# A causal attention block: the diagonal's first 64 queries of two heads share columns, and the token shift is mixed ahead of single products

## The chip, the cores and the metric

The kernel runs on one core of a Trainium2 chip. The metric is device time in microseconds (us) from start to end of the program on that core, as the median of several runs. Lower is better.

## What is computed

A batch of 8 sequences of 512 tokens and 128 channels goes through one attention layer with 16 heads of 8 channels, a residual and a layer norm, then through a channel mix with a token shift, a residual and a second layer norm. Cut to what matters:

```python
raw    = einsum('bhid,bhjd->bhij', q, k)
scores = alpha * tanh(raw / beta) + lam * hamming + lat      # two biases from 6-bit features
attn   = softmax(where(causal, scores, -inf))                # (8, 16, 512, 512), i >= j only
out    = einsum('bhij,bhjd->bhid', attn, v) @ out_w.T
x      = layernorm(x + out)
x_prev = concat([0, x[:, :-1]], axis=1)                      # the token before
xr     = mu_r * x + (1 - mu_r) * x_prev
xk     = mu_k * x + (1 - mu_k) * x_prev
r      = sigmoid(xr @ W_r.T)
kv     = square(relu(xk @ W_k.T)) @ W_v.T
x      = layernorm(x + r * kv)
```

## The kernel before

**Tiling.** A batch is one period of 20 steps. `P` is 128. For each head the kernel holds the scores transposed, keys on the partitions and queries on the columns. The 512 keys form 4 blocks (`jb`) of 128, and block `jb` is computed for queries `128*jb` to 512 alone: 512, 384, 256 and 128 columns, 1280 per head. Four heads form a quad, and the 5120 columns of a quad are packed into 5 pairs of PSUM banks of 1024 columns (`pair_units`), so a batch has 20 pairs. In each block the first 128 queries are the diagonal one, of which half is masked away.

**A pair's way.** TensorE makes the raw scores of pair `t+1` (`scores`, bf16 in three levels, contraction 72), ScalarE takes their tanh into `probs` (`tanh`), TensorE overwrites the bank with the two biases (`biases`, contraction 111), VectorE adds `alpha * tanh` to them (`main`, L1073), ScalarE takes exp (`exp`, L834, three steps later), GpSimd zeroes the masked triangle (`mask`, L962), and TensorE multiplies with the values (`weighted`, f32, four heads side by side in four strips of 32 output rows of the bank `sums`). There are three PSUM pairs for the raw scores and 10 buffers for `probs`.

**Side work.** Between the pairs run the side products of other batches through one bank (`side_bank`): for batch b+2 the transpose of x, q, k and the two feature products (`xT2`, `q2`, `k2`, `F2`, `G2`), for batch b+1 the values (`v1`), for batch b-1 the end of the layer (`oT0`, `oT1`, `aT`, `y`, `x1T`, `kk`, `rr`, `kv`). The tables `PREP_UNITS`, `VALUES_UNITS`, `POST_UNITS`, `VALUES_STEPS` and the `PREP`, `POST` and `SPLIT` tables of VectorE and GpSimd say in which step each engine does what; each engine runs its own list in order and waits on semaphores. `kk` and `rr` apply the token shift inside the product: the weights come twice, scaled by mu and by 1-mu (`w_k_mix`, `w_r_mix`), and the product of the token and that of the token before are added in PSUM.

**Three levels.** Each of Q, K, J and G is split in three bf16 levels: `hi` (VectorE cast), `rest` (GpSimd, the f32 remainder), `mid` (VectorE cast of it, L1112), `lo` (GpSimd). They go to DRAM and come back as the stacks `q_stack`, `k_stack`, `i_stack`, `j_stack` for the batch (SyncE, `write_rows` and `load_stacks`). The bias of a batch's first pair waits for the last of these loads.

**The ends.** Ahead of batch 0 stands a set-up with the first two batches' preparation. Batch 6 has no preparation left to do, batch 7 none and no values either, and after it comes the tail: the last pairs' exp, mask and product, and the end of the layer for batch 7, cut in halves.

## Time and profile before

| | us |
|---|---|
| median of 3 runs | 400.71 |
| lowest, highest | 400.51, 401.08 |
| the profiled execution | 402.91 |
| its span, first to last instruction | 401.2 |
| TensorE's granted clock, mean share of full speed | 0.979 |
| busy in the span: PE, DVE, ACT, POOL | 361.6, 333.0, 327.9, 229.8 |

PE is TensorE, PEld its weight loads, DVE is VectorE, ACT is ScalarE, POOL is GpSimd and SP is SyncE. Each row of a timeline is one instruction or a run of equal ones: its start, its length, the engine, the line, what it writes and reads, how many. In square brackets stands the idle time of the engine ahead of it, and what ended it. Starts of neighbouring rows tell more than their lengths on PE, because matmuls overlap.

### The profile page before, as it was taken

The page shows a single profiled execution, that of the slowest core. Times are in us where ns is not written, and L with a number is a line of the kernel's source. Part 1 is how long each engine was busy: PE and PEld are TensorE (multiplying, and loading weights), DVE is VectorE, ACT ScalarE, POOL GpSimd, SP SyncE. Part 2 cuts the span into 40 slices and gives each one's busy share as a digit, 9 for nine tenths or more (in the row PEclk, how much of TensorE's full clock was granted, in tenths as well). Part 3 has the DMA queues.
Part 4 walks back from the last instruction along what each step waited for, and adds up shares of the span by engine and source line. Part 5 has one row for each costly group of instructions (what it writes and reads, how often), then busy time and mean ns, then how long its engine had stood idle before and what let it go on. Part 6 is the DMA issues. An engine that isn't in the chain of part 4 may idle for free.

```text
span 401.2 us, 9042 instructions
## 1 busy us (share of the span) xinstructions
PE 361.6 (90%) x3045; PEld 209.1 (52%) x3045; DVE 333.0 (83%) x536; ACT 327.9 (82%) x367; POOL 229.8 (57%) x367
## 2 busy tenths in 40 slices
PE   7788878489999999999999999999989998989983
PEld 7473433134665565655564556455634564445572
DVE  4878979348999999989999999999978977797654
ACT  1216899538998999899999999899989998999811
POOL 4516557314578648765777567956684537344542
PEclk9999999859999999999999999999999999999998
DMA  4264786787613576357544763475337630100000
GB/s 127 72 192 144 233 235 177 205 236 174 155 59 116 159 196 176 100 157 189 154 139 128 203 158 116 146 204 159 117 116 209 174 95 2 54 26 3 2 28 26
DMA packets 37809, 53.76 MB, mean 134 GB/s; under 512 B 3523, under 2 KB 35267, under 8 KB 36191
## 3 DMA queue, kind: packets, MB, share of 16 engines
q1 hardware_dynamic: 32909, 50.83, 45.9%
q10 hardware_dynamic: 4865, 2.49, 2.5%
q8 instruction: 19, 0.31, 0.3%
q14 instruction: 16, 0.12, 0.1%
HBM read 38.69 MB, written 14.61 MB: 133 GB/s over the span
## 4 chain that ended last, share of the span: by engine, by line
PE 54%; DVE 12%; ACT 10%; issue 7%; DMA 6%; SPq 6%; POOL 4%; POOLq 0%; DVEq 0%; ACTq 0%
PE raw L521 25%; PE side_bank L521 13%; PE sums L521 12%; DMA i_stack<-hamming_i 5%; ACT probs L829 4%; DVE probs L1073 4%; ACT probs L834 4%; PE side_bank L613 3%; SPq L387 2%; POOL parts L975 2%; POOL res L1003 1%; DVE bn L1158 1%; DMA probs<-in_L_attn_hex_w 1%; SPq L403 1%; ACT k_act L846 1%
## 5 line engine op out<-in xcount | busy, mean ns | idle before, releaser
L1073 DVE SCALAR_TENSOR_TENSOR probs<-probs,scal,raw 128x1024 f32<-128x1024 f32 x160 | 202.3, 1273 | 35.6 <-PE raw L521 35.0
L829 ACT ACTIVATE probs<-raw 128x1024 f32<-128x1024 f32 x160 | 164.4, 1028 | 33.0 <-PE raw L521 30.6
L834 ACT ACTIVATE probs<-probs 128x1024 f32<-128x1024 f32 x160 | 169.8, 1063 | 0.3 <-DVE probs L1073 0.3
L962 POOL TENSOR_SCALAR_AFFINE_SELECT probs<-probs 128x256 f32<-128x256 f32 (+1 forms) x224 | 97.2, 450 | 114.0 <-ACT probs L834 113.6
L521 PE MATMUL raw<-i_stack,j_stack 111*128 111x384 bf16 (+3 forms) x512 | 97.8, 303 | 11.7 <-DMA i_stack<-hamming_i 7.8
L521 PE MATMUL raw<-q_stack,k_stack 72*128 72x384 bf16 (+3 forms) x512 | 97.8, 303 | 9.6 <-DVE probs L1073 7.5
L521 PE MATMUL sums<-probs,values 128*32 128x256 f32 (+2 forms) x1280 | 82.4, 384 | 0.4 <-POOL probs L962 0.4
L521 PEld LDWEIGHTS raw<-q_stack,k_stack 72*128 72x128 bf16 x512 | 42.4, 98 | 58.8 <-DVE probs L1073 27.4
L521 PEld LDWEIGHTS raw<-i_stack,j_stack 111*128 111x128 bf16 x512 | 41.4, 98 | 55.8 <-issue 22.6
L521 PEld LDWEIGHTS sums<-probs,values 128*32 128x32 f32 x1280 | 33.8, 109 | 30.2 <-issue 20.0
L975 POOL TENSOR_TENSOR parts<-whole,parts 128x512 bf16<-128x512 f32 x30 | 35.6, 1195 | 3.8 <-DVE parts L1112 3.1
L969 POOL TENSOR_TENSOR whole<-whole,parts 128x512 f32<-128x512 f32 x22 | 26.9, 1223 | 11.1 <-DVE parts L1107 11.1
L521 PE MATMUL sums<-ident 128*128 128x128 f32 x118 | 16.8, 296 | 1.6 <-POOL ident L941 1.6
L1112 DVE CAST parts<-whole 128x512 bf16<-128x512 f32 x31 | 18.2, 602 | 0.0
L521 PEld LDWEIGHTS sums<-ident 128*128 128x128 f32 x118 | 15.9, 211 | 3.0 <-POOL ident L941 1.6
L985 POOL TENSOR_TENSOR rstd<-var_eps,minus_half 128x4 f32<-128x4 f32 x14 | 14.7, 1047 | 1.2
L521 PEld LDWEIGHTS side_bank<-w_r_mix,x1T 128*128 128x128 f32 x112 | 13.1, 191 | 1.9 <-ACT k_act L846 1.9
L521 PE MATMUL side_bank<-w_r_mix,x1T 128*128 128x128 f32 x112 | 13.9, 277 | 0.0
L969 POOL TENSOR_TENSOR whole<-feats,parts 128x512 f32<-128x512 f32 x8 | 9.5, 1186 | 6.9 <-DVE parts L1107 6.9
L1003 POOL TENSOR_TENSOR res<-gated,x 128x512 f32<-128x512 f32 x7 | 9.0, 1289 | 7.6 <-DVE gated L1179 7.6
L1158 DVE BATCH_NORM_STATS2 bn<-res 128x6 f32<-128x128 f32 x56 | 12.2, 281 | 1.3 <-POOL res L1003 1.1
L521 PE MATMUL side_bank<-x1T,w_k_mix 128*128 128x512 f32 x28 | 13.2, 592 | 0.0
(154 smaller groups left out, 347.8 us busy)
## 6 DMA issues: line engine op xcount, KB each, us to landing
q_stack<-q_rows SPq DMA_DIRECT2D x21, 384.0 KB
k_stack<-k_rows SPq DMA_DIRECT2D x21, 384.0 KB
i_stack<-lattice_i SPq DMA_DIRECT2D x21, 288.0 KB
i_stack<-hamming_i SPq DMA_DIRECT2D x21, 288.0 KB
q_rows<-parts SPq DMA_DIRECT2D x8, 384.0 KB, 4.3
k_rows<-parts SPq DMA_DIRECT2D x8, 384.0 KB, 2.6
k_rows<-parts SPq DMA_DIRECT2D x8, 256.0 KB, 2.9
x_res<-in_L_attn_x SPq DMA_DIRECT2D x8, 256.0 KB, 3.0
```

Of the source, the lines that this page charges most:

```text
L521: return nc.tensor.matmul(o, lhsT, rhs, start=start, stop=stop, **kw)
L613: last = nc.tensor.transpose(o[:, n * P:(n + 1) * P], src(n), ident[:])
L829: nc.scalar.activation(pair_probs(t), raw[:, t % PSUM_PAIRS, :].rearrange("p (u i) -> p u i", u=2), ACT.Tanh).then_inc(tanh_done, 1)
L834: nc.scalar.activation(pair_probs(t), pair_probs(t), ACT.Exp).then_inc(exp_done, 1)
L962: last = nc.gpsimd.affine_select(out=v, in_=v, compare_op=ALU.is_ge, fill=0.0, base=0, pattern=[[0, v.shape[1]], [1, P]], channel_multipli ...
L969: nc.gpsimd.tensor_tensor(whole[:, kind, :], feats[:] if kind == J else whole[:, kind, :], parts[:, kind, 0, :], ALU.subtract).then_inc(re ...
L975: nc.gpsimd.tensor_tensor(parts[:, kind, 2, :], whole[:, kind, :], parts[:, kind, 1, :], ALU.subtract).then_inc(lo_done[kind], 1)
L985: nc.gpsimd.tensor_tensor(rstd[:], var_eps[:], minus_half[:], ALU.pow).then_inc(rstd_done, 1)
L1003: nc.gpsimd.tensor_tensor(res[:], gated[:], x1[:], ALU.add).then_inc(gate_done, 1)
L1073: v.scalar_tensor_tensor(out=o, in0=o, scalar=scal[:, 2:3], in1=raw[:, t % PSUM_PAIRS, :].rearrange("p (u i) -> p u i", u=2), op0=ALU.mult ...
L1112: v.tensor_copy(parts[:, kind, 1, :], whole[:, kind, :]).then_inc(mid_done[kind], 1)
L1158: v.bn_stats(bn[:, blk, :], res[:, blk, :]).then_inc(bn_done, 1)
```

## The change

**Packing.** A key block's last 64 keys are masked for the block's first 64 queries. The 128-key products therefore leave these queries out: a head has 448, 320, 192 and 64 columns, 1024 in all, two heads fill a pair, and a batch has 16 such pairs. What is left, 64 keys by 64 queries for each block and head, is a square. Eight heads' squares fill one pair (`is_square`, the 9th and the 18th of a batch): the first quad's on partitions 0 to 63, the second's on partitions 64 to 127, with the same columns. A batch has 18 pairs in place of 20. A square pair takes 32 products of 64 keys by 64 columns for the scores, 8 of 64 by 256 for the biases, and 16 for the values, with a value tile that holds the two heads below each other (`square_values`, filled by two more VectorE copies of 64 partitions). Its mask is a GpSimd product with a 0/1 tile (`triangle`, 128x1024); the others' masks are two selects of 2x64 columns each, in place of one or two of 2x128 or 4x128.

**Token shift.** GpSimd subtracts the token before from the token (`shift_diff`, 128x512), VectorE multiplies by mu and adds (`mixed`, twice), and `kk` and `rr` become one product each in place of two. The tail keeps the old form, with weights scaled by four VectorE instructions there.

**Splitting.** In the steady periods `mid` moves from VectorE's cast to GpSimd, which computes the same remainder a second time with a bf16 output.

**Order.** All tables are new for 18 steps. `sums_out` comes behind `main`, and GpSimd makes its constants in the set-up (`square_constants`).

```diff
-PAIRS_PER_QUAD = 5
-PAIRS = QUADS * PAIRS_PER_QUAD
+HALF_PAIRS = 9
+PAIRS = 2 * HALF_PAIRS
+SQUARE = 64
...
+                if is_square(t):
+                    for jb in range(JB):
+                        for r in range(4):
+                            for s in range(2):
+                                first_key = square_heads(t, s)[r] * T + jb * P
+                                at = 4 * SQUARE * jb + SQUARE * r
+                                last = mm(raw[SQUARE * s:SQUARE * (s + 1), t % PSUM_PAIRS, at:at + SQUARE],
+                                          k_stack[par][:, first_key:first_key + SQUARE],
+                                          q_stack[par][:, first_key:first_key + SQUARE])
+                else:
+                    for u, bank in enumerate(pair_units(t)):
+                        for h, jb, at in bank:
+                            n = T - jb * P - SQUARE
...
+                if is_square(t):
+                    squares = pair_probs(t).rearrange("p u i -> p (u i)")
+                    for jb in range(JB):
+                        for r in range(4):
+                            at = 4 * SQUARE * jb + SQUARE * r
+                            last = mm(sums[32 * r:32 * r + 32, jb * P:jb * P + SQUARE],
+                                      square_values[par][:, jb, 4 * k + r, :], squares[:, at:at + SQUARE],
+                                      start=False, stop=(jb == JB - 1), skip_group_check=True)
...
-                    mm(o, w_k_mix[0][:], x1T[:, 1:1 + T], stop=False)
-                    last = mm(o, w_k_mix[1][:], x1T[:, 0:T], start=False)
+                    pe.wait_ge(mix_done[1], pv + 1)
+                    last = mm(o, w_kT[:], mixed_in[1])
...
+                    nc.gpsimd.tensor_tensor(v, v, triangle[:].unsqueeze(1).broadcast_to([P, 2 * T // SQUARE, SQUARE]),
+                                            ALU.mult).then_inc(mask_done, 1)
...
+                for at in (0, SQUARE if p < 2 else P + SQUARE):
+                    block = v[:, :, at:at + SQUARE]
+                    last = nc.gpsimd.affine_select(out=block, in_=block, compare_op=ALU.is_ge, fill=0.0, base=SQUARE,
+                                                   pattern=[[0, 2], [1, SQUARE]], channel_multiplier=-1)
...
+            def mid(n, kind):
+
+                pool.wait_ge(hi_done[kind], n + 1)
+                nc.gpsimd.tensor_tensor(parts[:, kind, 1, :], feats[:] if kind == J else whole[:, kind, :],
+                                        parts[:, kind, 0, :], ALU.subtract).then_inc(mid_done[kind], 1)
...
+            def mixed(n, which):
+
+                dve.wait_ge(dif_done, n + 1)
+                v.scalar_tensor_tensor(out=mixed_in[which], in0=shift_dif, scalar=mu[:, which:which + 1],
+                                       in1=x1T[:, 0:T], op0=ALU.mult, op1=ALU.add).then_inc(mix_done[which], 1)
```

Before, PE in a steady period around the token shift's products (steps 16 and 17; the row with `w_k_mix` is `kk`, the one with `w_r_mix` is `rr`; the REGISTER_ALU rows set up waits):

```order
L521 MATMUL side_bank<-x1T,w_k_mix 128x512 x2
L521 MATMUL raw<-q_stack,k_stack 128x384
L521 MATMUL raw<-q_stack,k_stack 128x128
L521 MATMUL raw<-q_stack,k_stack 128x384
L521 MATMUL raw<-q_stack,k_stack 128x128
L562 REGISTER_ALU
L521 MATMUL raw<-i_stack,j_stack 128x512 x2
L622 REGISTER_ALU
L521 MATMUL side_bank<-w_r_mix,x1T 128x128 x8
```

Now, PE at the same products (steps 13 and 14; `k_act` and `r_tanh` hold the mixed input there):

```order
L540 MATMUL side_bank<-k_act,w_kT 128x512
L590 REGISTER_ALU
L540 MATMUL raw<-i_stack,j_stack 128x64
L540 MATMUL raw<-i_stack,j_stack 128x448
L540 MATMUL raw<-i_stack,j_stack 128x64
L540 MATMUL raw<-i_stack,j_stack 128x448
L540 MATMUL raw<-q_stack,k_stack 128x192
L540 MATMUL raw<-q_stack,k_stack 128x320
L540 MATMUL raw<-q_stack,k_stack 128x192
L540 MATMUL raw<-q_stack,k_stack 128x320
L664 REGISTER_ALU
L540 MATMUL side_bank<-w_rT,r_tanh 128x128 x4
```

The two products are halved, and each pair's blocks are 64 columns shorter, with 64-column blocks among them. The square pair's scores are one run of 32 small products, which stands on PE in steps 7 and 16 of a period, ahead of another pair's biases:

```order
L540 MATMUL side_bank<-woT,attnT 128x128 x4
L540 MATMUL raw<-q_stack,k_stack 64x64 x32
L590 REGISTER_ALU
L540 MATMUL raw<-i_stack,j_stack 128x192
L540 MATMUL raw<-i_stack,j_stack 128x320
```

Before, POOL from the first layer norm on (`x` is the normalised x1) to the third level of Q and the remainder of G, steps 11 to 14:

```order
L993 TENSOR_TENSOR x<-res,mean_var 128x512
L997 TENSOR_TENSOR x<-x,rstd 128x512
L959 REGISTER_ALU
L962 AFFINE_SELECT probs<-probs 128x4x128
L959 REGISTER_ALU
L962 AFFINE_SELECT probs<-probs 128x2x128
L959 REGISTER_ALU
L962 AFFINE_SELECT probs<-probs 128x2x128
L975 TENSOR_TENSOR parts<-whole,parts 128x512
L969 TENSOR_TENSOR whole<-whole,parts 128x512
```

Now, POOL from the same place, steps 9 to 11 (L1036 is `mid` of K, L1071 `shift_diff`, L1018 the square's mask):

```order
L1061 TENSOR_TENSOR x<-res,mean_var 128x512
L1065 TENSOR_TENSOR x<-x,rstd 128x512
L1014 REGISTER_ALU
L1023 AFFINE_SELECT probs<-probs 128x2x64 x2
L1036 TENSOR_TENSOR parts<-whole,parts 128x512
L1070 ISA
L1071 TENSOR_TENSOR gated<-x1T 128x512
L1014 REGISTER_ALU
L1018 TENSOR_TENSOR probs<-probs,triangle 128x1024
L1030 TENSOR_TENSOR whole<-whole,parts 128x512
L1043 TENSOR_TENSOR parts<-whole,parts 128x512
```

Between the layer norm and the next remainder GpSimd now also has the second level, the shift's difference and a mask over 1024 columns.

## Rows read from the trace of the kernel before

**Rows 1.** Windows: stretch and length, busy us per engine, clock, DMA share, GB/s
```profile
core 0: us, PE busy (x) PEld busy (x) DVE busy (x) ACT busy (x) POOL busy (x), PEclk, DMA share, GB/s
...
159.70:201.80 42.10, 41.01 (x360) 23.39 (x358) 39.47 (x60) 39.81 (x44) 29.14 (x45) 1.00 0.58 155
...
328.00:372.00 44.00, 40.55 (x365) 22.77 (x362) 33.93 (x47) 41.97 (x47) 20.37 (x39) 1.00 0.07 20
```

**Rows 2.** Timeline of PE where batch 1's first biases wait (start, length)
```profile
74.03 0.60 PE L521 MATMUL raw<-q_stack,k_stack 72*128 72x512 bf16 x2
81.85 1.03 PE L521 MATMUL raw<-i_stack,j_stack 111*128 111x512 bf16 x2 [7.21 <-DMA i_stack<-hamming_i]
```

**Rows 3.** Windows: the stretch of the low clock
```profile
77.00:90.50 13.50, 8.65 (x24) 3.85 (x24) 4.64 (x5) 3.83 (x4) 1.61 (x4) 0.51 0.88 243
```

**Rows 4.** Timeline of PE: `kk` in periods 1, 5 and 7
```profile
115.78 1.88 PE L521 MATMUL side_bank<-x1T,w_k_mix 128*128 128x512 f32 x4
...
284.36 1.88 PE L521 MATMUL side_bank<-x1T,w_k_mix 128*128 128x512 f32 x4
...
367.02 1.88 PE L521 MATMUL side_bank<-x1T,w_k_mix 128*128 128x512 f32 x4
```

**Rows 5.** Timeline of PE in steady periods: `rr`, scores, biases, products with the values
```profile
202.92 1.95 PE L521 MATMUL side_bank<-w_r_mix,x1T 128*128 128x128 f32 x16
...
207.24 0.60 PE L521 MATMUL raw<-i_stack,j_stack 111*128 111x384 bf16 x4
207.77 1.72 PE L521 MATMUL sums<-probs,values 128*32 128x256 f32 x24
209.42 0.61 PE L521 MATMUL raw<-q_stack,k_stack 72*128 72x512 bf16 x2
...
213.92 0.60 PE L521 MATMUL raw<-q_stack,k_stack 72*128 72x384 bf16 x4
214.35 0.60 PE L521 MATMUL raw<-i_stack,j_stack 111*128 111x512 bf16 x2
```

**Rows 6.** Timeline of PE in the set-up: the smallest products
```profile
12.53 0.46 PE L521 MATMUL raw<-twT,tr_sb 7*6 7x16 f32 x12
```

**Rows 7.** Groups of PEld by form, whole span: busy and mean ns behind the bar
```profile
L521 PEld LDWEIGHTS raw<-q_stack,k_stack 72*128 72x128 bf16 x512 | 42.4, 98 | 58.8 <-DVE probs L1073 27.4 <-issue 17.9 <-DVE w_k_mix L1238 0.2
...
L521 PEld LDWEIGHTS sums<-probs,values 128*32 128x32 f32 x1280 | 33.8, 109 | 30.2 <-issue 20.0 <-POOL probs L962 2.3
```

**Rows 8.** Timeline of ACT in period 7: one tanh to the next
```profile
363.50 1.04 ACT L829 ACTIVATE probs<-raw 128x1024 f32<-128x1024 f32 x1
364.41 1.07 ACT L834 ACTIVATE probs<-probs 128x1024 f32<-128x1024 f32 x1
365.35 1.04 ACT L829 ACTIVATE probs<-raw 128x1024 f32<-128x1024 f32 x1
```

**Rows 9.** Groups of DVE by form in the stretch 159.7 to 201.8
```profile
L1073 DVE SCALAR_TENSOR_TENSOR probs<-probs,scal,raw 128x1024 f32<-128x1024 f32 x20 | 25.4, 1272 | 1.7 <-PE raw L521 1.4 <-ACT probs L829 0.3
L1112 DVE CAST parts<-whole 128x512 bf16<-128x512 f32 x4 | 2.6, 663 | 0.0
...
L1107 DVE CAST parts<-whole 128x512 bf16<-128x512 f32 x3 | 1.4, 488 | 0.0
...
L1107 DVE CAST parts<-feats 128x512 bf16<-128x512 f32 x1 | 1.1, 1144 | 0.0
...
L1124 DVE COPY values<-side_bank 128x256 f32<-128x256 f32 x2 | 0.8, 420 | 0.0
...
L1170 DVE TENSOR_TENSOR res<-side_bank,x_res 128x512 f32<-128x512 f32 x1 | 0.7, 690 | 0.2 <-PE side_bank L521 0.2
```

**Rows 10.** Groups of POOL by form in the same stretch
```profile
L962 POOL TENSOR_SCALAR_AFFINE_SELECT probs<-probs 128x256 f32<-128x256 f32 x24 | 9.8, 425 | 8.6 <-ACT probs L834 8.6
L975 POOL TENSOR_TENSOR parts<-whole,parts 128x512 bf16<-128x512 f32 x4 | 4.8, 1204 | 0.0
...
L962 POOL TENSOR_SCALAR_AFFINE_SELECT probs<-probs 128x512 f32<-128x512 f32 x4 | 2.6, 640 | 1.8 <-ACT probs L834 1.8
```

**Rows 11.** Timeline of the tail: the last mask, and the last product with the values
```profile
379.86 0.64 POOL L962 TENSOR_SCALAR_AFFINE_SELECT probs<-probs 128x512 f32<-128x512 f32 x1 [0.63 <-ACT probs L834]
...
380.55 0.64 PE L521 MATMUL sums<-probs,values 128*32 128x256 f32 x8 [0.19 <-POOL probs L962]
```

226 lines of the change are left out of this document (132 added, 94 removed).

## The prediction

> **What bounds the kernel now.** I read the windows first. In a steady period (one batch, 42.1 us) PE is busy 41.0 us, ACT 39.8, DVE 39.5 and POOL 29.1 [rows 1]. PE has 1.1 us to spare, so PE sets the period, and ACT and DVE, 2.3 and 2.6 us behind, come next. In the last periods, without preparation, ACT is the busiest: 41.97 of 44.0 us [rows 1]. Second, the landmarks. The product `kk` stands in the same step of each period, at 115.78, 284.36 and 367.02 [rows 4]. Periods 1 to 5 are thus (284.36 - 115.78)/4 = 42.1 us each (2.1 a step), and the two behind them (367.02 - 284.36)/2 = 41.3. Third, the start: PE is through with batch 0 at about 74.6 and then stands 7.2 us, until the last load of batch 1's stacks has landed at 81.85 [rows 2], and the clock is at about half until 90.5 [rows 3]. What is saved ahead of 81.85 therefore only makes that wait longer. The sum is made against this execution's span of 401.2; its own time was 402.9 and the median is 400.7, so I take the difference of the spans off the median.
>
> **PE, a steady period: what goes.** Scores lose 256 columns for each of 16 heads, four blocks of 1024. Such a block takes 0.43 us from start to start (213.92 to 214.35 [rows 5]), so 1.7 us go. The biases lose the same, 1.7. In the product with the values four heads run side by side; the 24 matmuls at 207.77 are 896 columns of four heads (two blocks of 256, one of 384) and the next work starts 1.65 later [rows 5]. That is 1.55 without the change of tile shape (below), or 1.7 ns a column; 256 columns for four quads are 1.8. `kk` and `rr` are halved: (1.88 + 1.95)/2 = 1.9 [rows 4, 5]. Together 7.1 us go.
>
> **PE: what comes.** *Change of tile shape.* The biases at 207.24 need 0.43, yet the values' product behind them starts 0.53 later [rows 5]: 0.1 us for going from 128 output rows to 32, and I take as much for going back. Each of a square's two runs in 64-row tiles pays 0.2. *The square's scores*, 32 products of 64 by 64. The trace has no 64-row tile. From below: the two halves run side by side as the values' four strips do, and 16 times 64 columns at 0.43 ns are 0.43, so 0.6 with the changes. From above: a load (98 ns, the 128-wide row of [rows 7]) bare in front of each of the 32, 3.1, so 3.3. Twelve products of 16 columns took 0.46 [rows 6], 26 ns from start to start once the last one's own length is off; 32 of these are 0.8. I take 1.0, since that row is the nearest. *The square's biases*, 8 products of 256 columns: 4 x 107 ns side by side or 8 x 107 in a row, with the changes 0.6 to 1.05; I take 0.6. *Its product with the values*: two passes of 4 blocks of 64 columns, 0.45 if the columns count, 0.9 if the load (109 ns [rows 7]) does; I take 0.55. A square pair is 2.15, two are 4.3. *The 64-column blocks* of the other pairs (16 in the scores, 16 in the biases, 4 in the values' product) may be shorter than the load that runs beside them: 0 to 1.3 us a period, I take 0.5. Net: -7.1 + 4.3 + 0.5 = -2.3.
>
> A rule of the Trainium skill speaks against this part. TensorEngine Tiling (Restrictions) says that column tiling switches Fast Weight Load off, so 64-wide bf16 loads would not be as quick as the 128-wide ones here; TensorE: Matmul & The Clock Gate (LDWEIGHTS) puts such a load at columns/1.2 ns, by which an estimate is 53 ns for 64. By that the 32 scores would be 16 x 53 = 0.85 us if the halves overlap and 1.7 if not, in place of my 0.8. No row of this trace has such a load.
>
> **The other engines in the same period.** ACT: one tanh to the next is 1.85 us when it is not held up [rows 8], so two steps fewer are -3.7. DVE: two `main` fewer are -2.5, four casts fewer -2.65, two more value copies +0.8 (0.42 each, the price of the two that stand there), `mixed` twice between 0.69 (a two-input operation of that size) and 1.14 (the dearest of that size) each [rows 9], I take +1.8: net -2.5, to about 37. The same cast took 1.144 from `feats` and 0.488 from `whole` [rows 9], the first beside GpSimd work; with GpSimd busier the other three casts may cost up to 2 us more. GPSIMD Engine Reference (Specifications), of the Trainium skill, states such contention for DVE instructions in a two-port mode or with two SBUF inputs, and `mixed` has two; by it both `mixed` are at their upper price, 0.5 us over my sum. POOL: the selects leave 12.4 and bring 32 x 0.32 = 10.2 (two sizes, 425 and 640 ns, put 128 columns at about 0.32), two square masks of twice 1.2 are +4.8, four `mid` +4.8, `shift_diff` +1.2 [rows 10]: 29.1 becomes 37.7.
>
> **The period.** PE's 41.0 - 2.3 = 38.7, with its 1.1 of slack 39.8. Now DVE and POOL both stand at 37 to 38 with waits in between, where POOL had 13 us of air; I add 0.3: 40.1 us, 2.23 a step.
>
> **The whole.** Batch 0's two steps are hidden by the load that ends at 81.85; it would cost about 4 us if that cover were gone, and no instruction ahead of that load is moved (GpSimd's new constants, some 3 us, fall into its idle time in the set-up). From 81.85 to `kk` of period 1 it was 33.9 us for 15 steps, 2.3 over 15 x 2.1, the price of the low clock. Now 12 steps: 26.8 + 2.3, so `kk` at 111.0. Four periods of 40.1: 271.4. The next two were 41.3, where ACT's own work is 20 x 1.85 + 1.85 for `kk` and `rr` = 38.9, 2.4 less; now 18 x 1.85 + 1.85 + 2.4 = 37.6 each: 346.6. Behind the last `kk` there were 34.2 us (401.2 - 367.0). Now one step more stands there (+2.1), `kk` and `rr` are shorter (-1.9), and the last pair is a square: its mask is 2.4 instead of 0.64 on the path to the end [rows 11], and its products cost 0.2 more: 36.4. The tail's four weight instructions lie beside the last exp. The end is at 383.0, 18.2 earlier, and the median 382.5.
>
> **Rivals.**
> *GpSimd sets the period.* It works in order, and its list makes it wait: `mid` of G stands ahead of a mask and needs a VectorE cast that is two steps further on in VectorE's list; `shift_diff` waits for the copy of `x1T`, and behind it `mixed` holds VectorE, `main` and so the next scores. For it: 37.7 of 40.1. Against: most masks have two steps until they are needed. With 3.6 us of waits the period is 41.3: 1.2 x 4.7 periods more, 388.1.
> *The squares cost more than they free*, the slower side. Each of the 32 loads stays bare: 3.3 + 1.05 + 0.9 = 5.25 a square, 6.2 us more a period than in the sum, in about 5.7 periods (the last two have slack on PE): 382.5 + 35 = 418. It decides from 1.6 us over my 2.15, that is about 75 ns for each small score product in place of 26. Against: 32-row loads of four strips do overlap, or 24 matmuls with a mean load of 109 ns would not fit into 1.65 us.
> *Better.* The halves overlap fully (0.6 + 0.6 + 0.45), short blocks cost nothing, nobody else interferes: PE 37.2, and POOL's 37.7 with a us of waits sets 38.8: 1.3 x 4.7 off, 376.4.
> *It doesn't arrive.* The wait at 81.85 moves, because batch 1's stacks are written or fetched later, or the clock stays low longer after the now longer stand (about 11 us): 3 to 8 us more, up to 391.
>
> **How the numbers follow.** The forecast (378.5 to 387) 0.52, GpSimd 0.20, better 0.13, the start 0.06, squares too dear 0.08, and 0.01 for an end within 0.2% of before, about what a measurement of this kernel can tell from no change. Faster 0.90, same 0.02, slower 0.08. The range takes in the better case and GpSimd's with the unit costs' width (the squares' scores from 0.6 to 1.7 move the end by -4 to +8): 375 to 392.
>
> **What would show it.** Right: `kk` of periods 1 and 5 some 160 us apart; 32 small matmuls in about 1 us; the first biases of batch 1 still at about 82; a tanh-to-tanh step of 1.85 in period 7; POOL at 37 to 38 busy in a steady period. Wrong: a run of 32 that takes 2 us or more; VectorE's `mixed` or `main` held by `shift_diff`; PE's products with the values held by GpSimd's masks; PE idle for over 2 us in a steady period; or the load at 82 landing elsewhere.

## The result, and the profile after

| | before | after |
|---|---|---|
| median of 4 runs, us | 400.89 | 408.81 |
| lowest, highest | 400.51, 403.53 | 406.12, 411.22 |
| ratio, 95% interval | | 1.018 [1.010, 1.026] |
| profiled execution, its span | 402.91, 401.2 | 407.93, 406.2 |
| granted clock, mean | 0.979 | 0.949 |

The change made the kernel 1.8% slower (between 1.0% and 2.6%), where 382.5 us, 4.5% faster, was forecast. Its span of 406.2 is 23.2 us over the 383.0 of the sum.

First the windows of the kernel after, to be read against [rows 1]: two stretches from one `kk` to the next, the second without preparation (columns as there: busy us and instructions of PE, PEld, DVE, ACT, POOL, then the clock).

```profile
246.15:288.07 41.92, 38.65 (x495) 24.18 (x495) 39.42 (x59) 36.37 (x40) 36.49 (x57) 1.00 0.56 152
...
327.37:367.80 40.43, 35.88 (x483) 22.98 (x483) 34.76 (x51) 35.74 (x39) 22.39 (x46) 0.96 0.13 38
```

TensorE fell to 38.65 us a period, as forecast (38.7). The period stayed at 42, as it was [rows 4]. VectorE has 39.42 where 37 was forecast, and is now the busiest engine; the kernel before has 39.81 of it in a period cut in the same way (the table below), so VectorE lost 0.4 us and not 2.5. The groups of the page say where (busy us, mean ns, idle time before):

```profile
L1018 POOL TENSOR_TENSOR probs<-probs,triangle 128x1024 f32<-128x1024 f32 x16 | 37.8, 2365 | 11.5 <-ACT probs L874 11.5
...
L1257 DVE SCALAR_TENSOR_TENSOR k_act<-gated,mu,x1T 128x512 f32<-128x512 f32 x7 | 19.8, 2822 | 0.0
...
L540 PE MATMUL side_bank<-k_act,w_kT 128*128 128x512 f32 x14 | 8.4, 682 | 10.2 <-DVE k_act L1257 10.2
```

`mixed` for `kk` (it writes `k_act`'s buffer) takes 2.82 us in each of 7 periods, and PE stands 10.2 us in all for it. The timelines of the three engines at one of them (start, length):

```profile
243.19 2.82 DVE L1257 SCALAR_TENSOR_TENSOR k_act<-gated,mu,x1T 128x512 f32<-128x512 f32 x1
...
247.12 0.74 DVE L1257 SCALAR_TENSOR_TENSOR r_tanh<-gated,mu,x1T 128x512 f32<-128x512 f32 x1
...
243.11 2.35 POOL L1018 TENSOR_TENSOR probs<-probs,triangle 128x1024 f32<-128x1024 f32 x1
245.41 1.61 POOL L1030 TENSOR_TENSOR whole<-whole,parts 128x512 f32<-128x512 f32 x1
...
246.15 1.10 PE L540 MATMUL side_bank<-k_act,w_kT 128*128 128x512 f32 x2 [1.46 <-DVE k_act L1257]
```

The square's mask starts at 243.11 on GpSimd, `mixed` at 243.19 on VectorE. The mask ends at 245.46, `mixed` 0.55 us later; the other `mixed`, with nobody beside it, takes 0.74. GpSimd's next instruction takes 1.61, where the same form with nobody beside it takes 1.16: it in turn is held while `mixed` finishes. The other square of the period does the same to the cast of `feats` (`hi` of J):

```profile
264.02 1.84 DVE L1183 CAST parts<-feats 128x512 bf16<-128x512 f32 x1 [0.21 <-ACT feats L884]
...
263.22 2.36 POOL L1018 TENSOR_TENSOR probs<-probs,triangle 128x1024 f32<-128x1024 f32 x1
```

Not every VectorE instruction that reads SBUF is held. The statistics of the layer norm (one input) run beside six selects, and neither side is longer for it; all 56 of them took between 275 and 296 ns:

```profile
233.72 0.87 DVE L1237 BATCH_NORM_STATS2 bn<-res 128x6 f32<-128x128 f32 x4
...
233.57 1.51 POOL L1023 TENSOR_SCALAR_AFFINE_SELECT probs<-probs 128x128 f32<-128x128 f32 x6
```

The squares themselves are cheap. The 32 score products of one square, the next work, the 8 bias products of another with what follows, and the group of the weight loads for the scores of all squares:

```profile
103.54 0.69 PE L540 MATMUL raw<-q_stack,k_stack 72*64 72x64 bf16 x32
104.17 0.61 PE L540 MATMUL raw<-i_stack,j_stack 111*128 111x192 bf16 x4
...
173.10 0.63 PE L540 MATMUL raw<-i_stack,j_stack 111*64 111x256 bf16 x8 [2.57 <-issue]
173.66 0.72 PE L540 MATMUL raw<-q_stack,k_stack 72*128 72x64 bf16 x4
...
L540 PEld LDWEIGHTS raw<-q_stack,k_stack 72*64 72x64 bf16 x512 | 9.7, 115 | 3.5 <-DVE probs L1149 2.1 <-issue 0.4
```

32 products take 0.63 us from start to start and 8 take 0.56; the 32 matmuls of a square's product with the values take 0.57 (266.86 to 267.43). The row at 173.10 also shows a stand of 2.57 us that ends with "issue": PE waited for nothing that the profile shows. [Rows 1 to 5] have none like it. It is the first work behind the jump back of PE's loop.

The start, against [rows 2]:

```profile
19.02 3.08 DVE L1183 CAST parts<-whole 128x512 bf16<-128x512 f32 x1
...
19.88 1.84 POOL L995 MEMSET square_values<- 128x1024 f32 x2
...
27.04 0.94 PE L655 MATMUL side_bank<-ident,x_res 128*128 128x128 f32 x4 [4.16 <-DVE square_values L1203]
...
44.83 0.37 SPq L388 DMA_DIRECT2D k_rows<-parts  x1
...
86.90 1.03 PE L540 MATMUL raw<-i_stack,j_stack 111*128 111x64 bf16 x4 [3.58 <-DMA i_stack<-hamming_i]
```

Beside the new constants a cast takes 3.08 us, and batch 1's first biases stand at 86.90 in place of 81.85. The cast started beside a GpSimd `lo` that ended at 19.95, and it ended 0.38 us behind the second of the two memsets: between these two, which stand without a gap, VectorE did not get in. The tail, against [rows 11]: PE waits 1.80 us for the last square's mask, and behind that its clock is at 0.57 for 7.4 us.

```profile
383.63 0.65 PE L540 MATMUL sums<-probs,square_values 128*32 128x64 f32 x32 [1.80 <-POOL probs L1018]
...
384.60:392.00 7.40, 6.58 (x30) 5.75 (x31) 4.32 (x18) 0.77 (x2) 4.22 (x7) 0.57 0.12 38
```

### The profile page after: what moved, and what is told of

Same layout as the page of the kernel before. It is cut to its first block, busy times and chain, and to the rows that moved or that the text cites. A ratio compares the mean times of both kernels' runs of the same rounds, so it can differ in the third digit from the quotient of the medians.

```text
span 406.2 us, 11204 instructions
## 1 busy us (share of the span) xinstructions
PE 347.7 (86%) x4127; PEld 223.8 (55%) x4127; DVE 334.2 (82%) x532; ACT 299.6 (74%) x335; POOL 277.3 (68%) x451
## 4 chain that ended last, share of the span: by engine, by line
PE 29%; DVE 20%; issue 18%; POOL 14%; ACT 8%; SPq 5%; DMA 5%; POOLq 0%; DVEq 0%; ACTq 0%
PE raw L540 11%; PE sums L540 8%; DVE probs L1149 6%; PE side_bank L540 5%; DMA i_stack<-hamming_i 5%; ACT probs L874 4%; PE side_bank L655 4%; ACT probs L869 3%; POOL probs L1018 3%; POOL probs L1023 3%; SPq L406 2%; POOL x L1061 2%; DVE bn L1237 2%; POOL res L1077 2%; POOL whole L1030 2%
## 5 line engine op out<-in xcount | busy, mean ns | idle before, releaser
L1149 DVE SCALAR_TENSOR_TENSOR probs<-probs,scal,raw 128x1024 f32<-128x1024 f32 x144 | 182.5, 1272 | 26.1 <-PE raw L540 25.8
L869 ACT ACTIVATE probs<-raw 128x1024 f32<-128x1024 f32 x144 | 147.3, 1024 | 44.9 <-PE raw L540 39.6
L540 PE MATMUL raw<-i_stack,j_stack 111*128 111x64 bf16 (+4 forms) x640 | 90.6, 281 | 11.8 <-DMA i_stack<-hamming_i 5.2
L540 PE MATMUL raw<-q_stack,k_stack 72*64 72x64 bf16 (+4 forms) x1024 | 91.7, 240 | 10.4 <-DVE probs L1149 6.7
L1023 POOL TENSOR_SCALAR_AFFINE_SELECT probs<-probs 128x128 f32<-128x128 f32 x256 | 69.2, 300 | 36.3 <-ACT probs L874 36.2
L540 PEld LDWEIGHTS raw<-q_stack,k_stack 72*64 72x64 bf16 (+1 forms) x1024 | 50.4, 107 | 55.5 <-issue 21.7
L540 PE MATMUL sums<-probs,values 128*32 128x224 f32 (+3 forms) x1280 | 72.7, 357 | 0.7 <-POOL probs L1023 0.7
L540 PEld LDWEIGHTS raw<-i_stack,j_stack 111*128 111x128 bf16 (+1 forms) x640 | 47.4, 102 | 43.2 <-issue 19.1
L1018 POOL TENSOR_TENSOR probs<-probs,triangle 128x1024 f32<-128x1024 f32 x16 | 37.8, 2365 | 11.5 <-ACT probs L874 11.5
L1043 POOL TENSOR_TENSOR parts<-whole,parts 128x512 bf16<-128x512 f32 x30 | 37.9, 1271 | 5.3 <-DVE parts L1188 2.7
L1036 POOL TENSOR_TENSOR parts<-whole,parts 128x512 bf16<-128x512 f32 x15 | 17.5, 1166 | 15.2 <-DVE parts L1183 15.2
L1257 DVE SCALAR_TENSOR_TENSOR k_act<-gated,mu,x1T 128x512 f32<-128x512 f32 x7 | 19.8, 2822 | 0.0
L540 PE MATMUL side_bank<-k_act,w_kT 128*128 128x512 f32 x14 | 8.4, 682 | 10.2 <-DVE k_act L1257 10.2
```

The source lines that it names most:

```text
L540: return nc.tensor.matmul(o, lhsT, rhs, start=start, stop=stop, **kw)
L869: nc.scalar.activation(pair_probs(t), raw[:, t % PSUM_PAIRS, :].rearrange("p (u i) -> p u i", u=2), ACT.Tanh).then_inc(tanh_done, 1)
L1018: nc.gpsimd.tensor_tensor(v, v, triangle[:].unsqueeze(1).broadcast_to([P, 2 * T // SQUARE, SQUARE]), ALU.mult).then_inc(mask_done, 1)
L1023: last = nc.gpsimd.affine_select(out=block, in_=block, compare_op=ALU.is_ge, fill=0.0, base=SQUARE, pattern=[[0, 2], [1, SQUARE]], channel ...
L1036: nc.gpsimd.tensor_tensor(parts[:, kind, 1, :], feats[:] if kind == J else whole[:, kind, :], parts[:, kind, 0, :], ALU.subtract).then_inc ...
L1043: nc.gpsimd.tensor_tensor(parts[:, kind, 2, :], whole[:, kind, :], parts[:, kind, 1, :], ALU.subtract).then_inc(lo_done[kind], 1)
```

## The experiments

My theory behind the result was this: (A) a VectorE instruction that reads SBUF alone cannot work while GpSimd is inside an instruction, so the 2.35 us mask makes it that much longer, and VectorE sets the period. (The statistics above show that "reads SBUF alone" is too wide. What the runs show held are `mixed` and, in `e7_mask_on_dve`, a product, each with two SBUF inputs, and the casts from f32 to bf16.) The rivals: (B) GpSimd's added load or its order sets it; (C) two inputs of the mask are what hurts. All kernels are the changed one with the edit named, unless the text says otherwise. The table has what they gave. The period is that from `kk` of period 4 to that of period 5 (the clock was 1.00 in all of them), with the busy time in it.

| kernel | median us | ratio to before [95%] | period | PE | DVE | POOL |
|---|---|---|---|---|---|---|
| before | 400.9 to 402.1 | 1 | 42.11 | 41.36 | 39.81 | 29.10 |
| after | 408.81 | 1.018 [1.010, 1.026] | 41.92 | 38.65 | 39.42 | 36.49 |
| e1_const_early | 407.55 | 1.017 [1.007, 1.026] | 41.87 | 38.65 | 39.38 | 36.42 |
| e2_mask_waits | 401.82 | 1.004 [1.001, 1.008] | 41.22 | 38.51 | 38.35 | 36.03 |
| e3_both | 398.56 | 0.994 [0.989, 0.998] | 41.21 | 38.49 | 38.36 | 36.02 |
| e4_old_shift | 405.53 | 1.016 [1.010, 1.022] | 41.91 | 40.09 | 36.11 | 34.29 |
| e5_one_input | 392.05 | 0.972 [0.966, 0.978] | 39.53 | 38.17 | 37.02 | 34.05 |
| e6_hi_later | 397.24 | 0.986 [0.982, 0.990] | 40.10 | 38.06 | 36.99 | 36.24 |
| e7_mask_on_dve | 415.90 | 1.032 [1.026, 1.038] | 42.52 | 38.63 | 40.01 | 32.72 |
| e8_fills | 400.24 | 0.997 [0.994, 0.999] | 41.21 | 38.50 | 38.34 | 36.04 |
| e9_two_selects | 401.02 | 0.997 [0.993, 1.001] | 40.35 | 38.28 | 37.85 | 35.74 |
| e10_selects_hi_later | 397.31 | 0.985 [0.980, 0.991] | 39.71 | 38.36 | 36.47 | 36.24 |
| e11_tail_fill | 392.55 | 0.977 [0.973, 0.982] | 39.71 | 38.35 | 36.47 | 36.25 |
| e12_old_shift_selects | 402.48 | 0.999 [0.995, 1.003] | 40.79 | 39.65 | 34.75 | 34.31 |
| e13_lo_k_early | 393.12 | 0.979 [0.974, 0.984] | 39.73 | 38.37 | 36.49 | 36.30 |
| e14_mid_on_dve | 407.57 | 1.015 [1.009, 1.021] | 42.87 | 39.12 | 39.45 | 31.67 |
| e15_before_filled | 405.04 | 1.008 [1.005, 1.011] | 42.09 | 41.36 | 39.81 | 29.05 |
| e16_pe_unrolled | 387.91 | 0.965 [0.960, 0.969] | 39.72 | 38.29 | 36.48 | 36.26 |
| e17_before_unrolled | 401.26 | 0.999 [0.995, 1.003] | 42.10 | 41.40 | 39.82 | 29.07 |

Single executions of one kernel lie up to 5 us from their median (e6_hi_later: 392.35 to 401.19, with a mean granted clock from 0.967 down to 0.942). Where the whole is doubtful I go by the period: profiles of kernels with the same steady period agree to 0.02 us (before, e15 and e17; e3 and e8; e10, e11, e13 and e16).

### The start, and the mask behind `mixed`

`e1_const_early` has GpSimd make its constants ahead of the first `rest`:

```diff
+            square_constants()
             for kind in (J, K):
                 rest(0, kind)
                 lo(0, kind)
-            square_constants()
```

> One part of the changed kernel moved: GpSimd makes the square constants (square_constants) before its first remainder, where it stood idle from 5.4 to 12.4 us, instead of behind the second one, at 19.9 us. Theory A (a GpSimd instruction and a VectorE instruction that needs the same SBUF interface exclude each other; the cast at 19.0 us took 3.08 us instead of 1.21 because the constants ran then): the cast is back at about 1.2, batch 1's first biases start 2 to 4 us earlier than at 86.9, and the whole is 2 to 4 us shorter than the changed kernel (405 to 407). Theory B (the start is late because of the two new square_values copies and a period 0 with other order, not because of the constants): first biases stay at 86 to 87, the whole within 1 us of the changed kernel.

`e2_mask_waits` makes the square's mask of step 11 wait for `mixed`, `e3_both` has both edits:

```diff
+                    if post and t == 11:
+                        pool.wait_ge(mix_done[1], b)
+                        stand_alone(pool)
                     if t >= EXP_LAG or post:
                         mask(*lagged(b, t, EXP_LAG))
```

> One wait added to the changed kernel: in periods with a layer end, GpSimd starts the first square pair's mask only when VectorE is through with mixed for kk. Theory A (the mask over 1024 columns, two inputs, 2.35 us, locks VectorE's mixed out, which takes 2.82 instead of 0.74): mixed is at 0.74 to 0.8, PE's wait before kk (1.46) goes, and a steady period is 1 to 2 us shorter than 42.05, the whole 6 to 12 us shorter (397 to 403). Theory B (GpSimd's load of 36.5 us of 42 with its order sets the period; VectorE's long mixed is filled waiting): GpSimd loses about 1 us more per period, the period stays at 42 or grows by up to 1, the whole 408 to 415.

> Both edits: the constants early and the first square mask behind mixed. Theory A: the gains add, 8 to 16 us off the changed kernel, 393 to 401, which would be the kernel before or better. Theory B: no gain, 406 to 412. If only one of the two mechanisms is there, this run is within 1.5 us of the run that has that one edit alone.

Timelines: the cast of the set-up and the first biases of batch 1 in `e1_const_early`; then `mixed` and the mask in `e2_mask_waits`.

```profile
19.07 1.21 DVE L1183 CAST parts<-whole 128x512 bf16<-128x512 f32 x1
...
84.03 1.03 PE L540 MATMUL raw<-i_stack,j_stack 111*128 111x64 bf16 x4 [4.79 <-DMA i_stack<-hamming_i]
```

```profile
280.43 0.75 DVE L1260 SCALAR_TENSOR_TENSOR k_act<-gated,mu,x1T 128x512 f32<-128x512 f32 x1
...
282.74 1.63 DVE L1260 SCALAR_TENSOR_TENSOR r_tanh<-gated,mu,x1T 128x512 f32<-128x512 f32 x1
...
281.45 2.36 POOL L1018 TENSOR_TENSOR probs<-probs,triangle 128x1024 f32<-128x1024 f32 x1 [1.06 <-DVE k_act L1260]
```

The cast is back at 1.21 us as soon as the memsets are gone, and the biases come at 84.03, 2.9 of the lost 5.05 earlier. In the profiles of the changed kernel and its variants the biases stand at 86.3 to 88.1 with the late constants (five kernels) and at 84.0 to 86.2 where only the constants are early (nine), and at 81.4 to 82.9 in three profiles of the kernel before and its variants. So the constants are worth some 2 us, and the other 2 to 3 us of the start are not explained by them. The whole (407.55, forecast 405 to 407) did not show it beyond its interval. The wait brings the first `mixed` to 0.75, and the second, which now meets the mask's last 1.07 us, goes from 0.74 to 1.63: the hold follows the mask. VectorE lost 1.07 us and the period 0.70, less than the 1 to 2 us that I had expected. The whole gained 7.0 us. Of the 8.9 us between the two profiles, 4.2 lie in the four periods with preparation, 2.1 in the two behind them, 0.5 in the tail, and 2.1 ahead of the `kk` of period 1, of which 1.8 stand between the first biases and that `kk`, whose `mixed` the mask had held as well. `e3_both` came to 398.56, 10 us under the kernel after and inside the 393 to 401 of theory A; its two periods without preparation take 38.55 and 38.10 in place of 39.30 and 40.42.

### The packing alone

`e4_old_shift` takes the token shift back (weights scaled by mu in the set-up, `kk` and `rr` as double products, no `shift_diff`, no `mixed`):

```diff
-                    last = mm(o, w_kT[:], mixed_in[1])
+                    mm(o, w_k_mix[0][:], x1T[:, 1:1 + T], stop=False)
+                    last = mm(o, w_k_mix[1][:], x1T[:, 0:T], start=False)
...
-                    last = four(o, mixed_in[0], w_rT[:])
...
+                    for n in range(JB):
+                        mm(o[:, n * P:(n + 1) * P], x1T[:, 1 + n * P:1 + (n + 1) * P], w_r_mix[0][:], stop=False)
+                        last = mm(o[:, n * P:(n + 1) * P], x1T[:, n * P:(n + 1) * P], w_r_mix[1][:], start=False)
```

> The changed kernel with the token shift undone: kk and rr are two products each with weights scaled in the set-up, no shift_diff on GpSimd, no mixed on VectorE; packing, masks, splitting on GpSimd and the tables stay. PE has 1.9 us more work per batch, GpSimd 1.0 less, VectorE 3.6 less. Theory A (mixed behind the mask costs over 2 us of VectorE per period, more than the products save): a steady period of 40 to 41 us, the whole 4 to 10 us below the changed kernel (398 to 405), though PE does more. Theory B (GpSimd's masks and second level, not the token shift, set the period): 41.5 to 43 us per period, the whole 406 to 411. Theory C (PE is the bound): longer, 412 or more.

The period stayed at 41.91 with no `mixed` in it. Here PE is the busiest again (40.09 of 41.91), VectorE at 36.11. That is theory B's period (41.5 to 43) and not A's (40 to 41); the whole, 405.53, lies between the two. With PE as the busiest engine it doesn't decide between them, so this run alone told little of the cause, and the shift was worth nothing in the period while `mixed` was held.

### The length of the mask: one select, two selects, VectorE

`e5_one_input` masks with one select; the squares of the second quad stay unmasked.

```diff
-                    nc.gpsimd.tensor_tensor(v, v, triangle[:].unsqueeze(1).broadcast_to([P, 2 * T // SQUARE, SQUARE]),
-                                            ALU.mult).then_inc(mask_done, 1)
+                    nc.gpsimd.affine_select(out=v, in_=v, compare_op=ALU.is_ge, fill=0.0, base=SQUARE,
+                                            pattern=[[0, 2 * T // SQUARE], [1, SQUARE]],
+                                            channel_multiplier=-1).then_inc(mask_done, 1)
```

> The changed kernel with one edit: GpSimd masks a square pair with one select of 128x1024 (one input, no triangle tile) in place of the product with the triangle (two inputs). The second quad's squares, on partitions 64 to 127, so stay unmasked; no instruction is more or fewer. By the selects of 128 elements at 0.246 us apart it should take 8 x 0.246 = 2.0 us in place of 2.35. Theory A (VectorE's mixed and its cast hi J are held up because the product reads two SBUF inputs): mixed for kk falls from 2.82 to 0.75, the cast of feats beside the other square's mask from 1.83 to 0.4 to 1.1, VectorE's busy time in a steady period from 39.4 to 36.6 to 37.3, and the steady period from 42.0 to 40.2 to 41.0; the whole about 398 to 402. Rival B (any GpSimd instruction of that length holds VectorE up): mixed stays at 2.3 to 2.5, the period at 41.7 to 42.0, the whole 405 to 408. Rival C (mixed is released, but it is not what sets the period): mixed 0.75, period still 42.0.

```profile
238.45 1.60 DVE L1258 SCALAR_TENSOR_TENSOR k_act<-gated,mu,x1T 128x512 f32<-128x512 f32 x1
...
238.36 1.15 POOL L1018 TENSOR_SCALAR_AFFINE_SELECT probs<-probs 128x1024 f32<-128x1024 f32 x1
239.47 1.59 POOL L1031 TENSOR_TENSOR whole<-whole,parts 128x512 f32<-128x512 f32 x1
```

The select took 1.15 us, not the 2.0 that I had scaled from the narrow ones, and the whole fell by 17 us to 2.8% under the kernel before. But `mixed` was not set free: it takes 1.60 and ends 0.54 us after the select. An instruction with one input holds VectorE just as one with two does, for as long as it runs. Rival C fell, and with it my own wording in that expectation. The run leaves B open, because GpSimd also had 2.4 us less (34.05 for 36.49).

`e9_two_selects` closes it, with the full computation: two selects one after the other, with a wait between, so that GpSimd has about as much to do as with the product.

```diff
-                    nc.gpsimd.tensor_tensor(v, v, triangle[:].unsqueeze(1).broadcast_to([P, 2 * T // SQUARE, SQUARE]),
-                                            ALU.mult).then_inc(mask_done, 1)
+                    nc.gpsimd.affine_select(out=v, in_=v, compare_op=ALU.is_ge, fill=0.0, base=SQUARE,
+                                            pattern=[[0, 2 * T // SQUARE], [1, SQUARE]],
+                                            channel_multiplier=-1).then_inc(half_done, 1)
+                    pool.wait_ge(half_done, 2 * b + t // HALF_PAIRS + 1)
+                    stand_alone(pool)
+                    nc.gpsimd.affine_select(out=v[0:SQUARE], in_=v[0:SQUARE], compare_op=ALU.is_ge, fill=0.0, base=0,
+                                            pattern=[[0, 2 * T // SQUARE], [1, SQUARE]],
+                                            channel_multiplier=-1).then_inc(mask_done, 1)
```

> The changed kernel with one edit, and the full computation: the square's mask is made by two selects, one over all 128 partitions (masks 64 to 127) and, behind a wait for it, one over partitions 0 to 63, in place of the product with the triangle. GpSimd's time for it hardly changes: 1.15 + 0.1 to 0.2 + 1.15 = 2.4 to 2.5 us in place of 2.35 (1.15 as the one select of e5_one_input took). Theory A (VectorE is held until the GpSimd instruction that runs has ended, whatever its inputs): VectorE gets in between the two, so mixed for kk takes 1.6 to 1.9 in place of 2.82, the cast hi J 0.6 to 1.5 in place of 1.83, VectorE's busy time in a steady period is 37.0 to 38.2 in place of 39.4, the period 39.6 to 40.8 in place of 42.0, the whole 392 to 399. Rival B (GpSimd's total load sets the period; e5_one_input won because it took 2.4 us a period off GpSimd): period 41.8 to 42.2, whole 406 to 409. Rival C (two inputs matter by themselves): mixed 0.75, period 39.5.

```profile
244.14 1.60 DVE L1263 SCALAR_TENSOR_TENSOR k_act<-gated,mu,x1T 128x512 f32<-128x512 f32 x1
...
246.85 1.56 DVE L1263 SCALAR_TENSOR_TENSOR r_tanh<-gated,mu,x1T 128x512 f32<-128x512 f32 x1
...
244.06 1.14 POOL L1018 TENSOR_SCALAR_AFFINE_SELECT probs<-probs 128x1024 f32<-128x1024 f32 x1
245.37 1.37 POOL L1023 TENSOR_SCALAR_AFFINE_SELECT probs<-probs 64x1024 f32<-64x1024 f32 x1 [0.16 <-POOL probs L1018]
```

VectorE slips in between the two: `mixed` 1.60, VectorE 37.85, period 40.35 in place of 41.92, with GpSimd at nearly its old load (35.74, was 36.49) and the mask done later than before (2.68 us from its start, for 2.35). VectorE and the period are where A had them, and B's period of 41.8 to 42.2 is excluded. The whole is not where A had it: 401.02, over A's 392 to 399 and under B's 406 to 409. In its profile the `kk` of period 1 comes at 119.84, 2.95 us later than in the kernel after, so part of the gain was lost ahead of the steady periods.

`e7_mask_on_dve` moves the same product to VectorE, one step later (base `e1_const_early`):

```diff
+            def square_mask(b, t):
...
+                dve.wait_ge(exp_done, PAIRS * b + t + 1)
+                stand_alone(dve)
+                o = pair_probs(t).rearrange("p u (n i) -> p (u n) i", i=SQUARE)
+                v.tensor_tensor(o, o, triangle[:].unsqueeze(1).broadcast_to([P, 2 * T // SQUARE, SQUARE]),
+                                ALU.mult).then_inc(square_done, 1)
```

> e1_const_early with the square's mask moved from GpSimd to VectorE (the same product with the triangle, one step later; its own semaphore). GpSimd loses 2 x 2.35 us a period, VectorE gains two products of 128x1024, which by main (1.27 us for 128x1024) and by mixed (0.74 for 128x512) take 1.3 to 1.5 each. Theory A (hold-up by GpSimd's product): mixed 0.75 both, VectorE's busy 39.4 - 2.1 - 0.7 to 1.4 + 2.6 to 3.0 = 38.5 to 39.6, GpSimd 31.8; the period 40.5 to 41.7, and the tail falls by 1 us since its last mask takes 1.3 instead of 2.35; whole 400 to 404. Rival (VectorE alone is the bound at 94% of the period): period = busy/0.94 = 41 to 42, whole 403 to 407.

```profile
250.63 2.21 DVE L1160 TENSOR_TENSOR probs<-probs,triangle 128x1024 f32<-128x1024 f32 x1
...
209.06:254.55 45.49, 41.55 (x495) 25.69 (x495) 40.13 (x61) 36.63 (x40) 32.87 (x56) 0.93 0.49 138
254.55:297.07 42.52, 38.63 (x494) 24.07 (x495) 40.01 (x61) 36.35 (x40) 32.72 (x56) 1.00 0.55 147
```

My prices missed: the product itself is held (2.21 in place of 1.3 to 1.5), the `mixed` behind it too (1.64), VectorE comes to 40.0, and the period at full clock is 42.52, with the whole at 415.90 over both forecasts. PE stands 2.35 to 2.69 us ahead of each of these `kk`, and in three of the four periods its clock was lower (0.93 in the one shown); those took 45.5 to 46.6. GpSimd had 3.8 us less than in the kernel after, and all got slower.

### The other hold-up, and what is left

`e6_hi_later` is `e3_both` with the cast `hi` of J and `mid` of J one step later:

```diff
-            SPLIT = {2: [(hi, J)], 4: [(hi, Q)], 9: [(hi, K)], 14: [(hi, G)]}
+            SPLIT = {3: [(hi, J)], 4: [(hi, Q)], 9: [(hi, K)], 14: [(hi, G)]}
...
-            PREP = {2: [(mid, J)], 4: [(mid, Q), ...
+            PREP = {3: [(mid, J)], 4: [(mid, Q), ...
```

> e3_both (constants early, square mask behind mixed) with one more edit: VectorE's cast hi J and GpSimd's mid J stand one step later, behind the square's mask of that step. Theory A (the second hold-up in a period is this cast beside the other square's mask): the cast falls from 1.83 to 0.4 to 0.6, VectorE's busy time from 38.35 to about 37.0, the steady period from 41.2 to 40.2 to 40.7; 4 periods with preparation give 2 to 4 us, so 395 to 397. Rival (VectorE is not the bound of the period, its wait just moves): cast 0.42, period 41.0 to 41.2, whole 398 to 399. A third way: mid J, now later, delays GpSimd's chain rest, lo, and the loads: period above 41.2.

```profile
259.12 0.46 DVE L1186 CAST parts<-feats 128x512 bf16<-128x512 f32 x1
...
256.19 2.38 POOL L1018 TENSOR_TENSOR probs<-probs,triangle 128x1024 f32<-128x1024 f32 x1
```

The cast falls from 1.84 to 0.46, VectorE by 1.37 and the period by 1.11, to 40.10. That is the prediction's number, in part by luck: the second `mixed` is still held there (1.69), and PE has 38.06 and not 38.7. The whole is 397.24, just over the 395 to 397 of theory A. `e10_selects_hi_later` adds the two selects, `e11_tail_fill` also gives PE 10 idle products in the tail, ahead of the last square's values.

> e6_hi_later (constants early, square mask behind mixed, hi J a step later; 40.1 a steady period, 36.99 of VectorE in it) with the mask by two selects as in e9_two_selects. If hold-ups on VectorE are what is left: mixed 0.75 and 1.2 (in place of 1.69), VectorE 36.5, the period 39.6 to 39.9; the masks of the no-preparation periods likewise; whole 394 to 396.5. If the period is now TensorE's (38.05 busy in 40.1) and its waits for the last pairs: 40.0 to 40.1, whole 396.5 to 398.

Both `mixed` take 0.75 us (the median of seven each) and the period is 39.71, as the first forecast had it (39.6 to 39.9). The whole, 397.31, is no better than `e6_hi_later`.

```diff
+            for t in range(PAIRS - 3, PAIRS):
+                if t == PAIRS - 1:
+                    pe.wait_ge(scores_done, PAIRS * B - 2)
+                    busy(10, raw[:, 0])
+                weighted(B - 1, 1, t)
```

> e10_selects_hi_later with 10 idle products (1.1 us) on TensorE in the tail ahead of the last square's values. Theory (the tail's stretch of half clock behind its last mask comes from TensorE's idle time there): the tail falls from about 37.8 to 35.5 to 36.5 and the whole by 1 to 2. Rival (they only stand in the way): the tail and the whole the same or 0.5 longer.

Timelines of PE in the tail, first `e10_selects_hi_later`, then `e11_tail_fill`:

```profile
374.21 1.08 PE L540 MATMUL sums<-probs,square_values 128*32 128x64 f32 x32 [1.90 <-POOL probs L1023]
...
380.36 4.46 PE L540 MATMUL sums<-ident 128*128 128x128 f32 x24
```

```profile
367.61 2.50 PE L540 MATMUL raw<-ident 128*128 128x128 f32 x20
...
370.04 0.65 PE L540 MATMUL sums<-probs,square_values 128*32 128x64 f32 x32
...
374.43 2.84 PE L540 MATMUL sums<-ident 128*128 128x128 f32 x24
```

The fill is 20 matmuls (each f32 product is two) and takes 2.5 us, not the 1.1 of the expectation. Behind it the last square's values start 0.7 us later in the tail than without it (16.7 us behind the last `kk`, for 16.0), but from there to the end it takes 20.7 in place of 23.3: the same 24 matmuls, themselves idle products that the kernel has in its tail already, take 2.84 in place of 4.46 us. The tail is 37.4 in place of 39.3, less of a gain than expected. None of the five profiled kernels with the fill (e8, e11, e13, e14, e16) shows a half clock in the tail but for the last 3 to 5 us, where PE has nothing left to do; the kernel after and every profiled variant of it without the fill shows one. The whole fell by 4.8, more than the 1.9 of the tail; what of the rest is scatter of the clock elsewhere I can't tell.

`e8_fills` had tried more on `e3_both`: 18 idle products more in the set-up and, in the kernel that ran, 12 in the tail (24 matmuls, 2.9 us), where the expectation speaks of 17:

> e3_both with TensorE kept busy at two places where it stood idle ahead of a fall of its clock: 18 more idle products (2.0 us) in the set-up ahead of the transposes of x for batch 2, and 17 (1.9 us) in the tail ahead of the last square's values, for which TensorE waits 1.8 us for GpSimd's mask. Theory (the clock falls because TensorE stood idle there, and its half clock costs about half of each stretch): the tail goes from 38.6 to 35 to 36.5, the stretches of low clock behind 378 and at the start are gone, whole 394.5 to 396.5. Rival (the clock falls anyway, by what went before): tail and start unchanged or longer by up to 1 us, whole 398 to 400.

The tail went from 38.7 to 37.8, short of the theory's 35 to 36.5, and the whole was no better than `e3_both` (400.24 for 398.56, the rival's number): nothing shows that the fill in the set-up helped. `e15_before_filled` is the kernel before with the fill of 10:

> The kernel before, with 10 idle products on TensorE in the tail ahead of the last pair's values, as e11_tail_fill has them. Its profile shows no fall of the clock between 378 and 391, so nothing to be gained there: theory, within 0.3% of the kernel before; rival (the fill gains by itself what e11_tail_fill showed): 1 to 3 us faster.

It gave 405.04 us, 1.008 [1.005, 1.011], slower than either forecast. Its tail has full clock as long as PE works, as that of the kernel before, and there the products only stand in the way: they take 2.5 us, and the last product with the values comes 2.2 us later behind the last `kk` than in the kernel before. So the fill pays where the clock would fall, behind the changed kernel's long mask, and costs where it would not.

`e12_old_shift_selects` is `e10_selects_hi_later` without the token shift:

> e10_selects_hi_later with the token shift undone: weights scaled by mu in the set-up, kk and rr as double products, no difference on GpSimd, no mixed on VectorE. So it is the packing of the diagonal alone, with its side effects mended. TensorE has 1.5 us more in a period (40.1 by e4_old_shift), VectorE 1.5 to 2.5 less, GpSimd 1.0 less. Theory (TensorE bounds once VectorE is free): the period is 41.2 to 41.8 and the whole 399 to 402, so the shift is worth 1.3 to 1.7 a period once nothing collides. Rival (the remaining bound is common, about 40): period 40.0, whole within 1 us of e10_selects_hi_later.

The period is 40.79 (PE has 39.65 in it), where `e10_selects_hi_later` has 39.71: between the two forecasts. Mended, the shift is worth 1.1 us a period and 5 us in all. The packing alone, mended, takes 1.3 us off the steady period (42.11 to 40.79), and yet the whole can't be told from the kernel before (0.999); its profile loses at the start (first biases at 86.21), at the jump back (43.30 for that period) and in the tail (39.2).

`e14_mid_on_dve` gives `mid` back to VectorE, on `e11_tail_fill`, and with it spreads GpSimd's `rest` and `lo` over other steps:

```diff
-            SPLIT = {3: [(hi, J)], 4: [(hi, Q)], 9: [(hi, K)], 14: [(hi, G)]}
+            SPLIT = {3: [(hi, J)], 4: [(hi, Q)], 5: [(mid, J)], 6: [(mid, Q)], 9: [(hi, K)], 11: [(mid, K)], 14: [(hi, G)], 16: [(mid, G)]}
...
+            PREP = {3: [(rest, J)], 4: [(rest, Q)], 6: [(lo, J)], 7: [(lo, Q)], 10: [(rest, K)],
+                    12: [(lo, K)], 15: [(rest, G)], 17: [(lo, G)]}
```

> e11_tail_fill with mid of the steady periods back on VectorE (four casts of 0.4 to 0.6, two steps behind hi) and off GpSimd (four of 1.16). VectorE's busy time 36.4 + 1.7 to 2.4 = 38.1 to 38.8, GpSimd's 36.2 - 4.7 = 31.5. Theory (VectorE sets the period from about 37 on, by e6_hi_later's 36.99 at 40.1 and e3_both's 38.35 at 41.2): the period goes from 39.7 to 41.0 to 41.5, the whole 396.5 to 399. Rival (GpSimd's load, 91% of the period, holds VectorE up and sets it): the period 39.2 to 39.7, the whole 390 to 392.5.

```profile
247.05:289.92 42.87, 39.12 (x494) 24.03 (x495) 39.45 (x63) 37.38 (x42) 31.67 (x54) 1.00 0.55 153
```

4.6 us less on GpSimd, 3.0 more on VectorE, and the period is 3.2 longer, more than the 41.0 to 41.5 expected. Some of these casts were held too (two of the four `mid` take 1.27 and 1.24 us, for 0.5), so VectorE grew by more than I expected. Since GpSimd's order changed as well, the run speaks against its load as the bound, and only weakly for VectorE's. Over all kernels with `mixed` the period is VectorE's busy time plus 2.5 to 3.4 us and PE's plus 1.4 to 3.9; in e4 and e12, without it, PE's plus 1.8 and 1.1. VectorE is busier than PE only in the kernel after, e1, e7 and e14. In the kernels of about 40 us and less (e5, e6, e10, e11) PE has 1.1 to 1.9 us more than VectorE, and which of the two sets the period there is not shown.

### The start again, and PE's code

`e13_lo_k_early` is `e11_tail_fill` with GpSimd's `lo` of K for batch 1 ahead of the first mask:

```diff
-            FIRST = {1: [(lo, 1, Q)], 2: [(rest, 1, J), (rest, 1, G)], 3: [(lo, 1, K)], 4: [(lo, 1, J)], ...
+            FIRST = {1: [(lo, 1, Q)], 2: [(rest, 1, J), (rest, 1, G), (lo, 1, K)], 4: [(lo, 1, J)], ...
```

> e11_tail_fill with GpSimd's lo of K for batch 1 in step 2 of batch 0, ahead of the first mask, in place of step 3 behind it. Theory (SyncE's write of batch 1's k rows waits for that lo, which waits behind a mask whose exp comes at 39.8): the write goes from 41.5 to about 40, every load behind it and the first biases of batch 1 from 84.1 to 82.3 to 82.8, the whole by 1.3 to 1.8. Rival (the queue's transfers, not the write's start, set the end of that chain): first biases 83.8 to 84.1, the whole unchanged.

```profile
40.18 0.37 SPq L388 DMA_DIRECT2D k_rows<-parts  x1
...
81.95 0.69 PE L540 MATMUL raw<-i_stack,j_stack 111*128 111x64 bf16 x4 [3.98 <-DMA i_stack<-hamming_i]
```

In its profile the biases are at 81.95, where the kernel before has them. But the median (393.12) did not move, as the rival had it, and `e16_pe_unrolled`, with the same work there, has them at 83.78. Profiles of the kernel before differ as well (81.85, 81.37 in e15, 82.90 in e17), so an effect of 1 to 2 us at this place can't be read from one profile, and 2 us of the start stay unsettled.

`e16_pe_unrolled` is `e13_lo_k_early` with PE's loop written out, `e17_before_unrolled` the kernel before with the same edit:

```diff
-            with pe.Fori(1, B - 4, 2) as i:
+            for i in range(1, B - 4, 2):
                 period(i, 1, True, True)
                 period(i + 1, 0, True, True)
```

> e13_lo_k_early with TensorE's loop over the four steady periods written out, so that TensorE's code runs straight on and has no jump back; no product is more or fewer. In the changed kernel TensorE has 4127 matmuls in place of 3045, its instruction loads (queue q8) come to 35 in place of 19, and they go on through the loop's second pass, where the kernel before has none for 100 us. Theory (the loop's body no longer fits into what TensorE keeps of its code, and the jump back is what it stands 2.5 to 3 us for): the stand at 164 to 168 is gone, the distance of kk from period 2 to 3 goes from 42.2 or 44.0 to 39.7 to 40.2, the whole by 2.5 to 4: 389 to 390.5. Rival (code is loaded too slowly for the short products, jump or not): a stand of 1 to 3 us stays somewhere in periods 1 to 4, the whole 391.5 to 393.

> The kernel before with the same edit. It shows no such stand, so by the theory nothing is gained: within 0.3% of the kernel before, with about 26 to 30 instruction loads in place of 19. Rival (loads of code cost TensorE or the DMA queues something each): 0.5 to 2 us slower.

The queue of instruction loads in the stretch 150 to 257 (packets, MB), in the kernel before and in the one after; then the windows of two periods in `e16_pe_unrolled`:

```profile
q8 instruction: 1, 0.02, 0.1%
```

```profile
q8 instruction: 13, 0.21, 0.8%
```

```profile
152.44:192.26 39.82, 38.37 (x495) 24.16 (x494) 36.59 (x59) 36.28 (x41) 36.21 (x59) 1.00 0.61 168
192.26:232.01 39.75, 38.29 (x496) 24.16 (x495) 36.51 (x59) 36.29 (x41) 36.22 (x59) 1.00 0.61 171
```

In the kernel before there is one load of code in this stretch, with the jump back and the loop's second pass in it. In the one after there are 13. From the `kk` of period 1 to that of period 3, one pass of the loop, the traces record 1557 instructions of PE before (720 matmuls, 720 weight loads, the rest registers, semaphores and one branch) and 2085 after (987 and 988). PE stands 2.5 to 3.1 us at the jump in each profiled kernel that has the loop and the square pairs, and in none of the kernel before. Written out, the stand is gone, and the period across the jump takes 39.82 in place of 43.97 in `e13_lo_k_early`, where the clock fell to 0.96 with the stand. The loads themselves do not go away: 11 stand in the same stretch of `e16_pe_unrolled`, where PE has no idle time that ends with "issue". That the stand is PE's wait for its code is inferred from this, since the profile names no releaser. The whole went to 387.91, under the 389 to 390.5 expected, 3.5% under the kernel before and the best of all. The kernel before gains nothing by the edit: 401.26, 0.999 [0.995, 1.003], with 24 loads of code in place of 19.

## Why the prediction was wrong

By its own steps, against the marks of the profile (forecast, then measured): the first biases of batch 1 81.85, 86.90; `kk` of period 1 at 111.0, 116.89; four periods 160.4, 171.2; two more 75.2, 79.7; behind the last `kk` 36.4, 38.4. The excess is 5.05 + 0.85 + 10.8 + 4.5 + 2.0 = 23.2 us. Of the 10.8, 2.9 stand at the jump back and 7.9 in the four periods' own length; of the 4.5, `e3_both` gives 3.1 back. So the step named below as the one that failed makes about 11 of the 23.2 us, the start 5.9, PE's code 2.9, the tail 2.0, and 1.4 in the last two periods are not assigned.

**PE's sum was right**, 38.65 for 38.7, in part by luck. Cut from `kk` to `kk`, PE had 41.36 before and not the 41.0 of [rows 1], so it lost 2.7 and not 2.3. A square costs less than the 2.15 I took: 1.76, with 0.63 for the scores, 0.56 for the biases and 0.57 for the values, against 1.0, 0.6 and 0.55, the first two near their lower bounds. So the rival of dear squares, my only way to the slower side, was the wrong one: the sign came out as it said and by none of its reasons. Of the rule on loads in the Trainium skill, TensorEngine Tiling (Restrictions), this was the test. The trace agrees with it so far: the 64-wide loads took 115 ns on average, the 128-wide ones of the same operand 99. The time of the run was not set by them: it took 0.63 us, under the estimate of 0.85 for halves that overlap.

**The step that failed is VectorE's "net -2.5, to about 37".** I put the two `mixed` at 1.8, between the 0.69 and the 1.144 us of [rows 9], with the dearest operation of their size as the upper end. They took 2.82 + 0.74 = 3.56, and that dearest one, the cast from `feats`, went to 1.84: 1.76 + 0.70 = 2.46 us, as much as lies between 37 and 39.42. 1.144 was no price of a size. It was a cast beside a GpSimd instruction of 1.16 us (198.75 to 199.91, the cast from 199.05 to 200.19); in the steady periods of the kernel before GpSimd has none over 1.34, and the change brought one of 2.35. I had seen the cast beside GpSimd's work and allowed "up to 2 us more", outside the sum and for the other three casts, which stayed at 0.42 each, without asking how long the longest new neighbour is. The sentence on contention in the Trainium skill, GPSIMD Engine Reference (Specifications), was the right pointer; I had read it as a price of 0.5 us. The trace agrees with its condition of two SBUF inputs: `mixed` is held, and `main`, which reads one input from PSUM, takes 1.27 beside the same masks. The casts, with one input, are held too, and the statistics, with one, are not; whether the casts run in the two-port mode that it also names, no run here shows. e2, e6 and e9 show the mechanism and that the period follows it. With the cast out of the way the period was 40.10 (e6), with both 39.71 (e10), for a forecast of 40.1.

**"GpSimd sets the period" was wrong in its form.** GpSimd had 36.49 us, less than the 37.7 of the sum, and e14 and e7 took 3.8 to 4.6 us off it and were slower. As far as these runs show, it matters through the length of single instructions, not through its load.

**"No instruction ahead of that load is moved, ... they fall into its idle time" was wrong.** GpSimd's idle time is not VectorE's: the memsets held a cast for 1.9 us (e1), and moving them away took some 2 of the 5.05 us off the chain of loads. What the rest comes from stays open; batch 0's own order is new as well (`AHEAD_FIRST`), which the sentence overlooked. This is the rival "it doesn't arrive", priced at 3 to 8 us, as an addition to the other misses and not in their place.

**PE's code was in no step.** 1.4 times as many products a period (x495 for x362), though of fewer columns, cost 2.6 us at the jump back, and that period took 44.95 us where its neighbours took 42.25 and 42.06. Runtime: NRT & Kernel Launch (Instruction fetch mechanics), of the Trainium skill, says that a taken branch to a target outside the two pages that are held forces a load before execution goes on. e16 agrees with the load at the branch, with 4.15 us between the two kernels in that period (the stand and what the clock lost by it). With two pages of 16 KB the traces do not agree for PE: the kernel before jumps back over a pass of 1557 instructions with a single load of 16 KB in 107 us.

**The tail**: the mask's 2.4 us was in the sum. What was not is that PE, after standing 1.80 us for it, runs at half clock. The tail is 2.0 us over the sum; the fill took 1.9 us off the longer tail of e10 (39.3) and 0.9 off that of e3 (38.7).

## What to carry to other kernels

When work moves to GpSimd, look at the length of its longest instruction beside VectorE's casts and its instructions with two SBUF inputs, and not at its total: cut it in two, or place it beside work that reads PSUM. A price taken from a slow row of a fast group is a wait, and its length is that of the neighbour; ask what the neighbour will be. And where a change makes the same work out of more instructions, see in the queue of instruction loads whether the loop is still held.

## What the runs showed of the hardware

- `mixed` on VectorE and GpSimd's masks and remainders exclude each other in both directions: `mixed` ends 0.55 us after the GpSimd instruction it met, whether that took 2.35 us (two inputs) or 1.15 (one), and GpSimd's next one goes from 1.16 to 1.6 while `mixed` finishes. A cast behind two memsets without a gap got in only behind the second (3.08 us for 1.21). `BATCH_NORM_STATS2` on SBUF (275 to 296 ns, 56 times) and `main`, with one input from PSUM (1.27 us), are not held.
- A select of 128x1024 takes 1.15 us, the product of the same size 2.36. [Rows 10] would have said it: 425 ns for 256 columns and 640 for 512 are 0.84 ns a column, 1.07 us for 1024.
- 32 bf16 products of 64 columns with 64 output rows, in two halves of the output rows, stand 20 ns apart (0.63 us for all), though their weight loads take 115 ns each.
- With a PE loop of two periods of x362 products (1557 instructions of PE a pass) there is one load of code in 107 us; with one of x495 (2085) there are 13, of 16 KB each (0.21 MB), and PE stands 2.5 to 3.1 us at the jump.
